# Exchanges of a twelve-stage decoder: loads cut by columns over all 128 partitions, and the 16-wide attentions' stores and order changed

## The reference, cut to what matters

```python
x = _layernorm(x + _L0_attn_ref(x, ...), axis=-1)                 # stage 0
x = _layernorm(x + _L0_xattn_ref(x, ctx_4096, ctx_4096, ...))     # stage 1, cross
x = _layernorm(x + _L0_ffn_ref(x, ...))                           # stage 2
x = _layernorm(x + _L1_attn_ref(x, ...))                          # stage 3, 32 heads 16 wide, rotary
x = _layernorm(x + _L1_xattn_ref(x, ctx_4096, ctx_4096, mask...)) # stage 4, cross
x = _layernorm(x + _L1_ffn_ref(x, ...))                           # stage 5
x = _layernorm(x + _L2_attn_ref(x, ...))                          # stage 6, 32 heads 16 wide, biases
...                                                               # stages 7 to 9
x = _layernorm(x + _L3_xattn_ref(x, ctx_4096, ...))               # stage 10, latent
x = _layernorm(x + _L3_ffn_ref(x, ...))                           # stage 11
```

## Time and profile before

| | us |
|---|---|
| median of 3 runs | 2575.83 (2575.33 to 2578.24) |
| profiled execution | 2576.39 |
| its span | 2575.1 |
| its mean granted TensorE clock | 0.985 |
| first 16-wide stage, exchanges | 885 to 1049 |
| second 16-wide stage, exchanges | 1786 to 1951 |

### The profile page before, as it was taken

The page is one execution under the profiler, slowest core; times in us unless marked ns, Lnnn a source line. Parts: engine busy times, 40 slices in busy tenths (PEclk is TensorE's granted clock), DMA queues, the critical chain, the costliest instruction groups (busy, mean ns, idle before and its releaser), DMA issues.

```text
span 2575.1 us, 37687 instructions
## 1 busy us (share of the span) xinstructions
PE 2443.7 (95%) x13016; PEld 1541.7 (60%) x13016; DVE 1669.7 (65%) x3133; ACT 990.9 (38%) x3580; POOL 733.6 (28%) x755
## 2 busy tenths in 40 slices
PE   8999999999999788899999999999998998999998
PEld 7865666666655555456666666556664554555554
DVE  3487777777755776587777777565665744445565
ACT  0013444444444466434444444433555412323330
POOL 1037344443322111273444433222220221000002
PEclk9999999999999999999999999999999999999999
DMA  8552233222322255222233222222552020224430
GB/s 173 103 138 72 77 94 99 86 88 69 95 82 74 90 185 183 85 83 74 90 97 92 83 78 89 83 100 80 178 183 82 22 74 29 86 74 148 133 101 33
DMA packets 220382, 249.97 MB, mean 97 GB/s; under 512 B 49792, under 2 KB 165952, under 8 KB 218144
## 3 DMA queue, kind: packets, MB, share of 16 engines
q1 hardware_dynamic: 220192, 247.56, 32.0%
HBM read 161.49 MB, written 85.98 MB: 96 GB/s over the span
## 4 chain that ended last, share of the span: by engine, by line
PE 74%; DVE 10%; DMA 7%; SPq 3%; issue 2%; ACT 2%; POOL 2%; DVEq 0%; POOLq 0%; ACTq 0%
PE banks L752 12%; PE banks L840 12%; DMA scratch_latent_pt<-blocks_s 7%; PE banks L824 4%; PE banks L902 4%; PE banks L1521 3%; PE banks L868 3%; PE banks L303 3%; PE banks L720 3%; PE banks L2091 3%; PE banks L733 3%; SPq L2715 3%; PE banks L2142 3%; PE banks L2119 2%; PE banks L2161 2%
## 5 line engine op out<-in xcount | busy, mean ns | idle before, releaser
L947 ACT ACTIVATE E_x<-S_x,sm_x 128x128 f32<-128x128 f32 x512 | 199.2, 390 | 303.6 <-DVE sm_x L1121 303.6
L1183 POOL TENSOR_TENSOR QT<-QT,const 128x512 f32<-128x512 f32 x128 | 171.8, 1342 | 428.8 <-DVE turned L1001 428.8
L161 POOL TENSOR_TENSOR norm_spread<-norm_mv,const 128x1 f32<-128x1 f32 x96 | 20.8, 217 | 910.8 <-DVE norm_mv L157 910.8
L752 PE MATMUL banks<-xT,weights 128*128 128x512 f32 x512 | 237.2, 597 | 7.6 <-POOL weights L1178 5.8
L2583 ACT ACTIVATE E_s<-banks,top_s 128x128 f32<-128x128 f32 x512 | 180.5, 380 | 98.1 <-DVE top_s L2688 98.1
L1079 DVE TENSOR_TENSOR x<-banks,x 128x256 f32<-128x256 f32 (+1 forms) x288 | 147.2, 511 | 84.6 <-PE banks L840 78.6
L840 PE MATMUL banks<-weights,OT 128*128 128x256 f32 x768 | 193.8, 382 | 5.0 <-DVE weights L1062 5.0
L840 PEld LDWEIGHTS banks<-weights,OT 128*128 128x128 f32 x768 | 142.1, 189 | 66.4 <-issue 28.0
L954 ACT ACTIVATE OT<-banks 128x512 f32<-128x512 f32 x128 | 76.2, 595 | 256.7 <-PE banks L902 256.6
L1185 POOL TENSOR_TENSOR QT<-QT,turned 128x512 f32<-128x512 f32 x128 | 169.0, 1321 | 10.0
L752 PEld LDWEIGHTS banks<-xT,weights 128*128 128x128 f32 x512 | 95.0, 191 | 116.9 <-issue 105.7
(11 more groups left out here) (320 smaller groups left out, 4913.0 us busy)
## 6 DMA issues: line engine op xcount, KB each, us to landing
scratch_pt<-blocks_x SPq DMA_DIRECT2D x124, 256.0 KB, 2.0
PT<-scratch_pt SPq DMA_DIRECT2D x496, 64.0 KB, 2.0
scratch_latent_pt<-blocks_s SPq DMA_DIRECT2D x56, 512.0 KB, 3.6
PT_s<-scratch_latent_pt SPq DMA_DIRECT2D x224, 128.0 KB, 2.9
weights<-in_L_xwq SPq DMA_DIRECT2D x64, 256.0 KB, 3.9
weights<-in_L_xwo SPq DMA_DIRECT2D x64, 256.0 KB, 4.4
scratch_latent_pt<-blocks SPq DMA_DIRECT2D x30, 512.0 KB, 2.6
PT<-scratch_latent_pt SPq DMA_DIRECT2D x120, 128.0 KB, 2.9
```

Of the source, the lines that this page charges most:

```text
L752: mm = PE.matmul(to, left[:, k, head], moving, start=name in ("P1", "P2", "P4", "P5") and k == 0, stop=k == 1, skip_group_check=name in (" ...
L947: ins = AC.activation(head_of(e, j, u), scores_of(s, j, u), ACT.Exp, bias=sm[:, 0, j:j + 1], scale=1.0, accum_out=sm[:, 1, j:j + 1])
L1183: PO.tensor_tensor(four(to), four(to), spread(cos128, 4), ALU.mult).then_inc(*pool_step.one())
```

## The change

In all three kinds of stage the fetch is cut the other way: each of its four loads takes one i and fills a quarter of the columns of all 128 partitions of PT, where it took one j and filled 32 partitions. The bytes, the pieces' size and what lies where afterwards are the same.

In the 16-wide stages alone: the store is issued by ScalarE, behind the exps of the next round, and SP's program holds the fetches only. VectorE's divide goes behind the maxima. The rotary queries' cosine product waits for the product instead of the raw copy, and the raw copy waits for the cosine product.

```diff
@@ cross
-                        parts = x_scratch[u % 2].rearrange("(i p j n) -> j p i n", i=4, p=32, j=4)
-                        for j in range(4):
-                            SP.dma_start(flat(PT[u % 2])[32 * j:32 * j + 32, :].rearrange("p (i n) -> p i n", i=4), parts[j]).then_inc(*x_pt_in[u % 2].one())
+                        parts = x_scratch[u % 2].rearrange("(i p j n) -> i j p n", i=4, p=32, j=4)
+                        for i in range(4):
+                            SP.dma_start(flat(PT[u % 2])[:, P * i:P * (i + 1)], parts[i]).then_inc(*x_pt_in[u % 2].one())
@@ latent
-                        parts = l_scratch[u % 2].rearrange("(i p j n) -> j p i n", i=4, p=32, j=4)
+                        parts = l_scratch[u % 2].rearrange("(i p j n) -> i j p n", i=4, p=32, j=4)
                         rows = PT[u % 2][:, :, :, :].rearrange("p s h n -> p (s h n)")
-                        for j in range(4):
-                            SP.dma_start(rows[32 * j:32 * j + 32, :].rearrange("p (i n) -> p i n", i=4), parts[j]).then_inc(*l_pt_in[u % 2].one())
+                        for i in range(4):
+                            SP.dma_start(rows[:, 2 * P * i:2 * P * (i + 1)], parts[i]).then_inc(*l_pt_in[u % 2].one())
@@ 16-wide, ScalarE
                         if kind == "q":
-                            AC.wait_ge(*s_q(b + 1))
+                            AC.wait_ge(*s_qcos(b + 1))
...
+                    def store(r):
+                        AC.wait_ge(*s_blocks(r + 1))
+                        if r >= 2:
+                            AC.wait_ge(*s_pt_in[r % 2](4 * (r // 2)))
+                        AC.dma_start(s_scratch[r % 2].rearrange("(p n) -> p n", p=P), blocks[r % 2][:, :]).then_inc(*s_kept[r % 2].one())
...
+                        if 0 <= s - 1 < direct:
+                            store(s - 1)
                         if rotary:
                             if kind == "q":
                                 raw_copy(at, kind)
@@ 16-wide, VectorE
+                            DV.wait_ge(*s_q(b + 1))
                             if rotary:
-                                DV.wait_ge(*s_raw(b + 1))
...
                     for s in range(last):
-                        for r in mixes(s - 1):
-                            divide(r)
                         if s < ROUNDS:
                             DV.wait_ge(*s_score(s + 1))
...
+                        for r in mixes(s - 1):
+                            divide(r)
                         if 1 <= s <= ROUNDS:
                             turn_blocks(s - 1)
@@ 16-wide, SP
-                    def store(r):
...
-                        parts = s_scratch[r % 2].rearrange("(i p j n) -> j p i n", i=4, p=32, j=4)
-                        for j in range(4):
-                            SP.dma_start(PT[r % 3][32 * j:32 * j + 32, :].rearrange("p (i n) -> p i n", i=4), parts[j]).then_inc(*s_pt_in[r % 2].one())
+                        parts = s_scratch[r % 2].rearrange("(i p j n) -> i j p n", i=4, p=32, j=4)
+                        for i in range(4):
+                            SP.dma_start(PT[r % 3][:, 2 * P * i:2 * P * (i + 1)], parts[i]).then_inc(*s_pt_in[r % 2].one())
 
                     for r in range(direct):
-                        store(r)
                         fetch(r)
```

More of the change, by code:

```diff
@@ L2624, in late_drain @@
                                 DV.wait_ge(*s_score(4 * b - 4))
+                            DV.wait_ge(*s_q(b + 1))
                             if rotary:
-                                DV.wait_ge(*s_raw(b + 1))
                                 DV.scalar_tensor_tensor(QT[b % 2][:, :, :], four(work), 0.25, spread(cos16, 4), ALU.mult, ALU.mult).then_inc(*s_qcos.one())
                             else:
-                                DV.wait_ge(*s_q(b + 1))
                                 DV.scalar_tensor_tensor(QT[b % 2][:, :, :], four(work), 0.25, spread(bias4[:, :], P, at=2), ALU.mult, ALU.add).then_inc(*s_roped.one())
```

## The result

The changed kernel takes **2759.23 us** (median of 4 runs, 2754.88 to 2762.98), the kernel before on the same chip 2577.03 us (2575.33 to 2580.86). The ratio is 1.0704, 95% interval 1.0683 to 1.0725: slower by 182 us. The forecast was 2680 us in a range of 2615 to 2790. The sign and the cause held, and the time lies 79 us above the forecast.

What follows compares the result with a forecast made beforehand. The 16-wide exchange was taken as the bound, through SP's lap of store landing and issues, then four engines' time. 82 (16-wide) + 19 (cross) + 3 (latent) = +104 us on 2576.4 gave 2680 us, range 2615 to 2790.

Steps and rivals of the forecast that it cites:

- Four engines: All exchange loads: with a source outermost count of 4, each load runs on the same four DMA engines, not 16.
- Rival A: Loads still run on 16 engines; 16-wide stages gain at most 35 us of PE's idle time: 2541 us, chance 0.12.
- Engine time of 7.3 us per exchange: 16-wide stages on four engines: 6.0 us of loads at 47 ns a piece plus 1.3 of store, the shortest lap.
- Rival C: Four engines at the high price, 58 ns or more a piece, latent bound by SP's queue: 2791 us, chance 0.15.
- rival D: Four engines at the low price, 40 ns a piece: 2615 us, chance 0.10.
- So they don't run dry: 16-wide stages: SP's next loads follow 3.6 us after a landing, while the engines still work on the exchange between.
- +82: 16-wide stages: 56 exchanges, lap growing from 5.83 to 7.3 us, cost +82 us.
- ScalarE's wait: 16-wide store on ACT: back at a store 4.2 us after a landing, next landing after 7.3, so the wait is covered.
- Rival B: 16 engines, but ACT's wait at the store gives the gain back: no change, 2576 us, chance 0.03.
- Reordering at nothing: Divide behind the maxima and rotary product before the raw copy: worth 0 with the engines at the bound.
- Cross: +19 forecast: 124 cross exchanges: loads land 2.1 us later, 26 margins are shorter, shortfalls of +19 us (ends +8 and +28).
- Latent: 30 latent exchanges, store and loads on SP's queue: lap 8.9 us against 8.7, +3 us (0 to +27).

Runs made afterwards that it cites:

- the lap of 12.85: Changed kernel with each 16-wide load split in two of 64 partitions, so the source's outermost count is 2: 3011.58 us, ratio 1.1679 to the kernel before.

## Why the prediction was right in sign and cause, and 79 us short

**Four engines: right.** It was a judgement from the source's outermost 4. The 10,080 missing closing packets fit it to the packet, two closing packets appear where the count is 2, and with a count of 128 the cost disappears. The DMA share agrees: in a stretch of the changed kernel with loads only (999 to 1001.5) the records fill 27.3% of 16 engines, four engines' worth and a little overlap, though four loads are under way; so they share the same four.
```profile
q1 hardware_dynamic: 243, 0.24, 27.3%
```
Rival A, 16 engines and faster, is out for this kernel. The rule of the Trainium skill, "DMA: Bandwidth & Descriptors", in the section on the semaphore's 16, agrees: the slowest dimension of both patterns, here 4 against 128, decides, also where the short side is the one in DRAM.

**Engine time of 7.3 us per exchange: right as a floor, in part by luck.** With four scratches the lap is 7.35 and 7.17 us. By the share of busy time, which the forecast used, the 47 ns of a 1 KB piece were a little low: window share times 16 engines is 0.35 x 16 x 220 = 1232 us for 26.4 exchanges, 46.7 each, and without the store's 128 x 160 ns some 51 ns a piece (50 in the records of single packets). That would give 7.7 to 7.8 us, more than the measured 7.35, because the records overlap. Counted by the rate instead, the window 999 to 1001.5 has 235 pieces and 8 closing packets in 2.5 us on four engines, one piece per engine every 43 ns, with which an exchange takes 5.4 + 1.3 = 6.7 us. The 47 ns lie between the two readings, and that they hit the lap is in part luck: no run tells what fills the 0.4 to 0.6 us from 6.7 to the laps seen. Rival C's 58 ns and rival D's 40 ns were not seen, but a full queue comes near the 40.

**"So they don't run dry": the step that failed.** The working took a landing of 3.6 us for the store "beside other loads" from the earlier trace rows. That landing was seen with 16 engines, where the loads ahead are 32 pieces per engine. On four engines they are 128. The packets of the store issued at 985.05 show what follows, in the windows 985.05 to 987.5, 987.5 to 988.95 and 988.95 to 991.3 (q10 is ScalarE's queue, q1 SP's):
```profile
q10 hardware_dynamic: 108, 0.39, 39.1%
q1 hardware_dynamic: 220, 0.22, 26.9%
...
q1 hardware_dynamic: 116, 0.11, 24.0%
...
q10 hardware_dynamic: 36, 0.13, 13.6%
q1 hardware_dynamic: 103, 0.11, 12.6%
```
By 987.5 the store is through on the twelve engines without loads (12 x 9 packets). On the four others it has none until 988.95, while loads issued before it go first, and then its last 36 packets share the engines with further pieces of loads. A queue of its own doesn't take it past the loads already there: 6.4 us to landing at the median. The loads of the same scratch wait for that landing, and the next store into that scratch waits for these loads. The ring 6.5 + 1.65 + 8.6 us over two exchanges takes 8.4 us each, 1.0 us and more above the lap with four scratches. For part of that the engines stand still: from 991.47 to 992.84 no packet of the two queues is under way, and such a pause of some 1.0 us comes once in two exchanges. For the rest they run, but more slowly than with four scratches; what slows them isn't shown. That is 28 x (8.33 - 7.35) + 28 x (8.33 - 7.17) = 60 us of the 63 by which the 16-wide stages passed their +82 (73 + 72 = 145). Four scratches took 56 us off the time, which shows it. The leg that the prediction had wrong is the store's landing, 3.6 us against 6.5. By estimate, the same ring with 3.6 would have been 3.6 + 1.65 + 8.6 = 13.9 us over two exchanges, 6.9 each, below the 7.3 of the engines; so adding up the ring would not have been enough, the landing had to be taken behind four times as many pieces.

**ScalarE's wait: right.** At 985.02 the mix starts on the landing, at 985.05 the store goes out, 0.03 us later; nothing on ScalarE is late. Rival B never arose: with old loads the time falls by 21 us.

**Reordering at nothing:** 2556.62 against 2555.92 beside the old loads, where it might have been part of rival A's gain. Beside the new loads, for which the forecast stands, it wasn't run alone.

**Cross: +19 forecast**, 13 measured alone and some 10 in the whole. TensorE's idle time ahead of the matmuls of line 902 is 11.8 us, most of it in the stages' last exchanges, as the count of margins said. Its size was too high: counted again to the start of these matmuls, with the same 3.3 us from the first issue, 16 margins are under 2.1 us, the last eight of each stage, and their shortfalls add up to 11 us.

**Latent: mis-sized**, +3 forecast, 24 in the traces and 26 alone. A lap of 8.9 us was forecast, 7.3 of them engine time. Four stores of latent, the 14th and the 30th before, then the same two with only the latent loads changed:
```profile
2353.85 0.34 SPq L2050 DMA_DIRECT2D scratch_latent_pt<-blocks  x1
...
2491.02 0.34 SPq L2050 DMA_DIRECT2D scratch_latent_pt<-blocks  x1
...
2358.71 0.32 SPq L2050 DMA_DIRECT2D scratch_latent_pt<-blocks  x1
...
2515.86 0.45 SPq L2050 DMA_DIRECT2D scratch_latent_pt<-blocks  x1
```
The 16 laps between them take 9.82 us each instead of 8.57, and that is 20 us; the 13 laps ahead of them are as long as before, so not all 30 exchanges pay. The rest comes behind the last of these stores, where the last loads land later. In the lap of the timeline above, the packets of store and loads run from 2387.16 to 2395.01, 7.85 us, and then none is under way until 2396.71. That pause, 1.7 us from lap to lap, is close to the 1.6 us taken as fixed. The mis-sized term is the time on the four engines, about 8 us where 7.3 were taken. With the 16-wide stores on SP it is the same: pauses of 1.7 us in laps of 9.8. Here the queue runs empty in each lap, which it doesn't with four scratches, where 7.35 us are enough; that this is the reason isn't shown.

**The signs to look for.** Packets, as forecast. Landing of loads over 6 us: the last one 8.6. Stores 7.3 us apart: 8.33. Wait at line 2511 from 95 to near 180 us: 300. The 95 us were misread as TensorE's own wait, which was 37.2 us and became 137.9; in the two stages before TensorE idled 35 us in all. DMA share below 0.57: 0.35. The clock fell from 0.93 and 0.99 to 0.82 and 0.86 of 2.4 GHz where TensorE idles more, and to 0.72 at the lap of 12.85; TensorE is in no piece of the ring above, so the slower clock costs nothing there.

**Rival A's gain** was put at 35 us at most, all of TensorE's idle time in these stages. With 16 engines and the store on ScalarE it is 21. TensorE is busy 121.84 of 139 us there. What holds the last 14 us wasn't tried and stays open.

## What to carry to other kernels

In these runs the shorter outermost dimension set a load's engines (2 and 4), although it was the one on the side in DRAM: before turning a transfer round, read both patterns, and lay the scratch out so that both have many rows outermost (32 and 128 here kept all 16 engines). When a transfer goes on fewer engines, add up not only the engine time per lap but each ring of buffers it is part of, with landings as they are behind the queued loads: a landing read at 16 engines doesn't hold at four. Closing packets told the number of engines here: four small packets per load with a count of 4, two with 2, 16 with 128.

## What the runs showed of the hardware

- A store on a queue of its own doesn't go past loads that another queue has already put on the same engines: 6.4 us to land beside 512 pieces of loads on four engines, 3.6 to 3.7 on 16. In the one looked at, its first packets on the four engines came about 3 us after those on the twelve free ones, and from then on it shared them with pieces of loads.
- The issue of a load on SP took 0.43 us with 16 engines (1.73 for four) and 0.51 us with four.
- Packet records overlap on an engine: on two engines they add up to 13.6 us in a lap of 12.85, and with loads alone they fill 13.5% of 16 engines. So the DMA share overstates engine time. On two or four engines a 1 KB piece has a record of 46 to 52 ns, and in a full queue one starts on an engine every 43 to 44 ns.
- Loads to 128 partitions and to 32 differ little in the time of a piece (54 and 58 ns for 1 KB), and land after 2.2 and 2.9 us. The Trainium skill, "SBUF — State Buffer", section on the DMA port swizzle, has 32 partitions reach half of the 16 ports; for these loads no factor of that size shows.
